# Two feed-forwards of a macaron block: packed expert rows instead of dense passes for five of eight experts

## The chip, the cores and the metric

One core of a Trainium2 chip. The metric is the device time of one execution of the whole program in microseconds (us), median of three runs.

## What is computed

The input x has 8 batches of 512 tokens of 128 numbers, all fp32. Three residual steps follow each other:

```python
x = x + 0.5 * ffn(layernorm(x))
x = x + attention(layernorm(x))        # 16 heads of 64
x = x + 0.5 * ffn(layernorm(x))        # the same weights again
```

The feed-forward has two shared experts, which every token passes, and eight routed ones, of which each token uses two. An expert keeps at most 1280 (token, choice) pairs, counted in token order; what comes later is dropped:

```python
scores = softmax(x @ gate_w.T); topk_w, topk_idx = top_k(scores, 2)
topk_w = topk_w / (topk_w.sum(-1) + 1e-20)
keep = pos_tok < capacity                       # capacity = 1280 of 8192 pairs
comb = zeros(N, 8).at[arange(N), topk_idx].add(topk_w * keep)
eo_e = (silu(x @ we_gate_e.T) * (x @ we_up_e.T)) @ we_down_e.T      # for each expert e
y = sum over e of eo_e * comb[:, e]
sh = silu(x @ ws_gate.T) * (x @ ws_up.T) @ ws_down.T
return y + sh
```

## The kernel before

Tokens live in SBUF as `x_tok` (128 partitions are 128 tokens; 8 batches of 4 tiles of 128). Each engine has its own instruction list and runs it in order; semaphores tie them together. `setup_sync` (line 161 on) queues all loads on SP. Then come `ffn("f1")`, `attention()` and `ffn("f2")`, one behind the other on every engine.

The feed-forward (`ffn`, lines 277 to 751) goes batch by batch, and in a batch through ten groups k: the two shared experts and all eight routed ones, each on all 512 tokens, whichever expert a token has chosen. Tokens are transposed once a batch (`front`, L347), so columns are tokens. A group on PE is `gate_up` (L375): six fp32r matmuls of 512 columns. Each fp32 factor is split into a high and a low fp32r part, and three products make one. The gate result goes through silu on ACT (L496), the product with the up result is taken on DVE (`gated`, L635). For a routed expert PE spreads the combine weight of each token over the partitions by one bf16 matmul (`weights`, L410), and DVE multiplies by it (`weighted`, L643). ACT makes the high part of the hidden values (L505), POOL the low part (`hidden_low`, L728), and PE adds three down matmuls (`project`, L418) into one PSUM bank Y that collects all ten groups. At the end of a batch ACT copies Y with the factor 0.5, PE transposes it back (L427) and DVE adds it to `x_tok` (`residual`, L650). `groups` (L307) is the loop over b with k written out; `project` runs four groups late (LAG_Y), so that the other engines keep up.

Layer norm (`norm_stage`, 16 stages, L259 to L265) and routing (`route_stage`, 20 stages, L555 to L616) are chains of small DVE instructions. Tables written by hand (`NORM_AT`, `ROUTE_AT`) lay some stages in each group. Routing of batch b needs logits in token rows: PE multiplies (L355), ACT copies, PE transposes (L362). The top two are found by comparing all pairs of experts (L576 to L586, 256 columns), positions in an expert's queue by matmuls with a triangular matrix (`positions`, L382 to L387). The combine weights are split in three bf16 parts, transposed and kept as `comb_t`.

In the last batch of feed-forward 1, `follow` calls lay the first steps of attention between the groups (`early_pe`, `early_act`, `early_dve`). Attention itself (L851 on) runs in periods of one pair of heads, 64 of them and three before and after. It starts once all eight residuals are done (`ffn1["x_done"]`).

## Time and profile before

| | us |
|---|---|
| median of three runs | 1410.64 (1409.23 to 1411.74) |
| the profiled execution | 1412.86, of which the span from first to last instruction is 1410.8 |
| PE busy, share of the span | 1297.9, 92% |
| DVE | 1000.4, 71% |
| POOL | 926.1, 66% |
| ACT | 703.9, 50% |
| mean granted clock of TensorE | 0.978 of full |

Busy times are those of instructions that compute. Matmuls are pipelined and their ends are modelled: what a matmul costs is better read from the distance of two starts. A name such as `work` or `turn` can stand for several things in turn, since buffers are shared: in the feed-forward `work` holds the hidden values and `qk_h`, `qk_l` their parts.

### The profile page before, as it was taken

To read this page: it belongs to the slowest core of one execution; us is meant where nothing else is said; L and a number is where in the kernel's file an instruction comes from. 1 tells how busy PE (TensorE), PEld (TensorE's weight loads), DVE (VectorE), ACT (ScalarE), POOL (GpSimd) and SP (SyncE) were. 2 spreads that over 40 slices of the span, in tenths; PEclk is the share of its full clock that TensorE was granted. 3 is DMA by queue.
4 is the path that set the end of the run, shared out by engine and by line. 5 is a ranking of instruction groups with operands and counts; after the bars stand their busy time and mean duration, and the time that the engine had idled before them with its cause. 6 is when DMAs were issued, how large, how long until landed. Compare 5 with 4: busy or idle time off the path is not lost.

```text
span 1410.8 us, 25300 instructions
## 1 busy us (share of the span) xinstructions
PE 1297.9 (92%) x8258; PEld 828.9 (59%) x8258; DVE 1000.4 (71%) x1900; ACT 703.9 (50%) x1042; POOL 926.1 (66%) x684
## 2 busy tenths in 40 slices
PE   4999889689999999999999999999999937988997
PEld 2666666346656656666566566566566525666665
DVE  7889988687666666666666666666666426998896
ACT  3565555245455555555555545545545404555553
POOL 0444444577888888888888788788888512444444
PEclk9999999899999999999999999999999967999999
DMA  6000000123233232232232332332332210000000
GB/s 206 1 0 0 0 0 0 30 46 69 48 68 68 48 69 65 51 69 61 55 69 57 59 69 51 65 69 47 69 69 47 39 24 0 8 7 15 7 7 16
DMA packets 101418, 61.71 MB, mean 44 GB/s; under 512 B 75280, under 2 KB 84016, under 8 KB 101072
## 3 DMA queue, kind: packets, MB, share of 16 engines
q1 hardware_dynamic: 101328, 60.52, 19.8%
q8 instruction: 56, 0.92, 0.3%
q14 instruction: 34, 0.28, 0.1%
HBM read 24.30 MB, written 2.62 MB: 19 GB/s over the span
## 4 chain that ended last, share of the span: by engine, by line
PE 68%; DVE 8%; issue 3%; DMA 1%; DVEq 0%; POOL 0%; ACT 0%; SPq 0%; POOLq 0%; ACTq 0%
PE banks L919 16%; PE banks L902 13%; PE banks L934 6%; PE banks L878 6%; PE banks L843 6%; PE banks L907 4%; PE banks L375 4%; PE banks L943 4%; PE banks L862 3%; PE banks L418 2%; PE banks L885 1%; PE banks L410 1%; DVE xn L265 1%; DVE neg_max L1064 1%; DVE work L643 1%
## 5 line engine op out<-in xcount | busy, mean ns | idle before, releaser
L728 POOL TENSOR_TENSOR qk_l<-work,qk_h 128x512 fp32r<-128x512 f32 x160 | 206.3, 1293 | 301.2 <-ACT qk_h L505 299.8
L1064 DVE TENSOR_REDUCE neg_max<-banks 128x2 f32<-128x1024 f32 x256 | 313.4, 1224 | 102.5 <-PE banks L878 96.3
L1000 ACT ACTIVATE work<-banks 128x1024 f32<-128x1024 f32 x256 | 250.1, 1025 | 168.3 <-PE banks L907 168.3
L1148 POOL TENSOR_TENSOR turn<-turn,side_turned 128x512 f32<-128x512 f32 x128 | 160.7, 1276 | 129.1 <-DMA side_turned<-side 129.1
L919 PE MATMUL banks<-work 128*64 128x512 f32 x1024 | 233.8, 598 | 0.0
L1142 POOL TENSOR_TENSOR turn<-turn,fenc 128x512 f32<-128x512 f32 x128 | 162.4, 1291 | 12.6 <-DVE side L1057 8.9
L1153 POOL TENSOR_TENSOR qk_l<-turn,qk_h 128x512 fp32r<-128x512 f32 x128 | 162.1, 1289 | 0.9 <-ACT qk_h L1005 0.9
L1158 POOL TENSOR_TENSOR work<-work 128x1024 f32<-128x1024 f32 x64 | 153.1, 2392 | 6.2 <-PE banks L919 6.2
L919 PEld LDWEIGHTS banks<-work 128*64 128x64 f32 x1024 | 67.8, 136 | 132.8 <-issue 110.0
L505 ACT ACTIVATE qk_h<-work 128x512 fp32r<-128x512 f32 x160 | 100.6, 629 | 71.5 <-DVE work L643 62.1
L375 PE MATMUL banks<-x_hi,gu_hi 128*128 (+1 forms) x320 | 133.5, 417 | 2.6 <-DVE work L635 2.2
L375 PE MATMUL banks<-x_hi,gu_lo 128*128 (+1 forms) x320 | 128.9, 403 | 0.0
L375 PE MATMUL banks<-x_lo,gu_hi 128*128 (+1 forms) x320 | 127.6, 399 | 0.0
L878 PE MATMUL banks<-qk_h 64*128 64x512 f32 x512 | 116.7, 452 | 11.3 <-DVE neg_max L1064 8.3
L496 ACT ACTIVATE o_t<-banks 128x512 f32<-128x512 f32 x160 | 94.7, 592 | 63.8 <-PE banks L375 54.0
L1070 DVE TENSOR_TENSOR shift<-banks,own_rows 128x512 fp32r<-128x512 f32 x64 | 44.2, 691 | 111.0 <-PE banks L885 111.0
L643 DVE TENSOR_TENSOR work<-turn,banks 128x512 f32<-128x512 f32 x128 | 87.4, 684 | 35.2 <-PE banks L410 29.1
L1005 ACT ACTIVATE qk_h<-turn 128x512 fp32r<-128x512 f32 x128 | 80.5, 629 | 53.6 <-POOL turn L1148 53.5
L902 PE MATMUL banks<-qk_h 64*128 64x512 f32 x512 | 101.9, 395 | 1.4 <-DVE side L1057 1.4
L1057 DVE TENSOR_TENSOR turn<-banks,rope_t 128x1024 f32<-128x1024 f32 x63 | 77.1, 1224 | 36.6 <-PE banks L843 35.5
L902 PE MATMUL banks<-qk_h,qk_l 64*128 64x512 f32 x512 | 101.3, 392 | 0.0
L902 PE MATMUL banks<-qk_l,qk_h 64*128 64x512 f32 x512 | 101.3, 392 | 0.0
(149 smaller groups left out, 2517.6 us busy)
## 6 DMA issues: line engine op xcount, KB each, us to landing
side_turned<-side SPq DMA_DIRECT2D x256, 128.0 KB, 3.1
rec_all<-rec_d SPq DMA_DIRECT2D x128, 128.0 KB, 3.0
x_tok<-in_x SPq DMA_DIRECT2D x8, 256.0 KB, 5.8
out<-x_tok SPq DMA_DIRECT2D x8, 256.0 KB, 2.3
work<-in_w_gate_up SPq DMA_DIRECT2D x1, 1280.0 KB, 6.6
work<-in_w_qk SPq DMA_DIRECT2D x1, 1024.0 KB, 7.1
den_d<-den_rows SPq DMA_DIRECT2D x64, 4.0 KB
den_c<-den_d SPq DMA_DIRECT2D x64, 4.0 KB, 1.9
```

Of the source, the lines that this page charges most:

```text
L375: ins = nc.tensor.matmul(dst[:], w[:, j + k, :], of_batch(a, b), start=(n == 0), stop=(n == 2))
L643: nc.vector.tensor_tensor(hid[:, k % NH, :], prod[:, k % 2, :], C[k % 2][:], ALU.mult).then_inc(s["hidden"], 1)
L728: nc.gpsimd.tensor_tensor(hid_lo[:, k % 2, :], hid[:, k % NH, :], hid_hi[:, k % 2, :], ALU.subtract).then_inc(s["hid_lo_ready"], 1)
L878: ins = nc.tensor.matmul(M2[:, h, :], qk_h[OWN[h], g % SETS, Q, qt * P:(qt + 1) * P], qk_h[OWN[h], g % SETS, K, :], start=True, stop=True)
L902: nc.tensor.matmul(S[kt][:, h, :], k[OWN[h], g % SETS, K, keys], q[OWN[h], g % SETS, Q, :], start=(i == 0), stop=False)
L919: ins = nc.tensor.matmul(O[OWN[h], :], v_all[:, kt, n * DH:(n + 1) * DH], pt[:, g % 2, kt, h * T:(h + 1) * T], start=(kt == 0), stop=(kt = ...
L1000: nc.scalar.activation(pt[:, g % 2, kt, :], S[kt].rearrange("p h q -> p (h q)"), ACT.Exp, scale=QSCALE).then_inc(s["probs"], 1)
L1064: nc.vector.tensor_reduce(neg_max[:, g % 2, qt::DH], M2, AX.X, ALU.max, negate=True).then_inc(s["maxes"], 1)
L1142: nc.gpsimd.tensor_tensor(turn[:, g % 2, part], turn[:, g % 2, part], fenc[:], ALU.add).then_inc(s["with_fourier"], 1)
L1148: nc.gpsimd.tensor_tensor(turn[:, g % 2, part], turn[:, g % 2, part], side_turned[:, part], ALU.add).then_inc(done, 1)
L1153: return nc.gpsimd.tensor_tensor(qk_l[:, g % SETS, part], turn[:, g % 2, part], qk_h[:, g % SETS, part], ALU.subtract)
L1158: nc.gpsimd.tensor_tensor(pt[:, g % 2, 0, :], pt[:, g % 2, 0, :], pt[:, g % 2, 1, :], ALU.add).then_inc(s["first_sum"], 1)
```

## The change

Shared experts and the routed experts 0 to 2 stay dense, on all tokens. Experts 3 to 7 run on packed rows: the normalised row of each token is written for each of its two choices to a list in HBM (`xs_d`) by an indirect DMA of GpSimd, 128 rows a time, at the place `slot_id` that routing works out; rows that belong to a dense expert or are over capacity get a place beyond the list's end and are not written. Each row carries two more numbers, the row where its result goes and its weight (ROW = 130). SP reads the list of an expert (1280 rows) into `xe`, PE transposes it, and the expert runs in three parts of 512, 512 and 256 columns (`PART_TILES`). ACT scales the result rows by their weights (`move`), GpSimd writes them to `ys_d` by their row numbers (`give_back`), and at the end SP reads `ys_d` back in token order for both choices, and DVE adds both (`combine`). The lists are filled first by SP (`fill`): `xs_d` with rows whose destination is out of bounds, `ys_d` with zeros.

The order of work is a list of 55 units. The first 30 are dense; the last ten dense ones lie two by two ahead of the three parts of each packed expert:

```python
+def ffn_units():
+    dense = [("dense", b, g) for c in range(CHUNKS) for gs in (range(NSH), range(NSH, NSH + DENSE))
+             for b in range(CB * c, CB * (c + 1)) for g in gs]
+    units = dense[:len(dense) - BESIDE]
+    rest = dense[len(dense) - BESIDE:]
+    for k in range(SPARSE):
+        a, b, c = (("sparse", PARTS * k + n, NSH + DENSE + k) for n in range(PARTS))
+        units += [rest[2 * k], rest[2 * k + 1], a, b, c]
+    return units
```

Down products are single fp32 matmuls with the hidden values as weights, so the result stands in token rows; DVE adds it to `x_tok` with 0.5 (shared) or the combine weight (dense experts), and nothing is transposed back. The three-part combine weights, the weight rows and the high and low parts of hidden values and down weights are gone, with POOL's elementwise work. Layer norm and routing take a chunk of two batches at once; the top two are found by two maxima with a tie rule. Logits are taken with the tokens as weights.

```diff
-            def pool(pool):
-                def hidden_low(b, k, before):
...
+                def send(c):
+                    pool.wait_ge(s["xn_twice"], c + 1)
+                    pool.wait_ge(s["routed"], c + 1)
+                    for t in range(CT):
+                        for way in range(TOPK):
+                            nc.gpsimd.indirect_dma_start(
+                                xs, bass.IndirectOffsetOnAxis(slot_id[:, c % 2, way, t:t + 1].bitcast(U32), 0),
+                                rows_out[:, c % 2, way, t, :], None, bounds_check=SPARSE * CAPACITY - 1,
+                                oob_is_err=False).then_inc(sent[c % 2], 16)
+                def give_back(n):
+                    pool.wait_ge(s["y_moved"], n + 1)
+                    for j, t in enumerate(part_tiles(n)):
+                        nc.gpsimd.indirect_dma_start(
+                            ys_d, bass.IndirectOffsetOnAxis(xe[:, n // PARTS % 2, t, D:D + 1].bitcast(U32), 0),
+                            ys[:, n % YS, j * P:(j + 1) * P], None, bounds_check=TOPK * B * T - 1,
+                            oob_is_err=False).then_inc(returned[n % YS], 16)
...
+                def fetch(k):
+                    if k >= 2:
+                        for n in range(PARTS * (k - 1) - YS, PARTS * (k - 1)):
+                            at_least(sp, returned[n % YS], 16 * slot_rows(n))
+                    sp.dma_start(xe[:, k % 2], xs[k * CAPACITY:(k + 1) * CAPACITY]...).then_inc(in_xe[k % 2], 16)
+                def fetch_back(b):
+                    if b >= YIN:
+                        sp.wait_ge(s["x_done"], b - YIN + 1)
+                    for way in range(TOPK): ...   # 256 KB each into y_in
+                for n in range(2):
+                    sp.wait_ge(sent[n], 16 * 2 * CT * (CHUNKS // 2))
+                for k in range(SPARSE):
+                    fetch(k)
+                for n in range(S - YS, S):
+                    sp.wait_ge(returned[n % YS], 16 * slot_rows(n))
+                for b in range(B):
+                    fetch_back(b)
...
-                    for n, (w, a) in enumerate(((down_hi, hid_hi), (down_lo, hid_hi), (down_hi, hid_lo))):
-                        ins = nc.tensor.matmul(Y[:], w[:, k, :], a[:, k % 2, :], ...)
+                    for t in range(width(i) // P):
+                        tok = slice(t * P, (t + 1) * P)
+                        for m in range(summed):
+                            j = summed - 1 - m
+                            ins = nc.tensor.matmul(y_bank(i)[:, tok], hid[:, (i - j) % NH, tok], down_w[:, g - j, :],
+                                                   start=(m == 0), stop=(m == summed - 1))
...
+                def period(i):                     # PE
+                    if i < N:
+                        gate_up(i)
+                    c, q = chunk(i)                # six periods a chunk
+                    if 0 < c < CHUNKS and q == 0:
+                        logits(c)
+                    if c < CHUNKS and q == 4:
+                        positions(c)
+                    if front_at(i) is not None:
+                        front(front_at(i))
+                    if gathered_at(i) is not None: # two units ahead of a packed part
+                        gathered(gathered_at(i))
+                    if 0 <= i - LAG < N:
+                        down(i - LAG)
...
+                def combine(b):                    # DVE
+                    dve.wait_ge(in_y[b % YIN], 32 * (b // YIN + 1))
+                    if b == 0:
+                        dve.wait_ge(s["y_added"], results(N, "dense"))
+                    xb = x_tok[:, b].rearrange("p t d -> p (t d)")
+                    steps.link(tt(xb, xb, y_in[:, b % YIN, 0].rearrange("p t d -> p (t d)"), ALU.add))
+                    tt(xb, xb, y_in[:, b % YIN, 1].rearrange("p t d -> p (t d)"), ALU.add).then_inc(s["x_done"], 1)
```

Comments in this fence mark what the shortened lines are. `setup_sync` queues `fill(sp, 0)` behind the loads of x and `fill(sp, 1)` behind attention's weights, 7.5 MB each, both ahead of feed-forward 1's `fetch`. The weight splits of gate and up are in two halves, the second at unit 4; attention's are in the last units (`early_act`, `early_dve`). Attention's first norm, projection and rotation are laid between the combines of feed-forward 1 (`joined`).

## Rows read from the trace of the kernel before

**Rows 1.** Stretches: us, busy of PE, PEld, DVE, ACT, POOL; clock, DMA share, GB/s.

```profile
0.00:20.00 20.00, 6.93 (x16) 3.29 (x17) 10.23 (x44) 7.58 (x9) 0.20 (x4) 1.00 0.90 279
60.00:260.00 200.00, 178.70 (x829) 127.20 (x828) 174.42 (x490) 108.30 (x184) 89.46 (x70) 1.00 0.01 3
180.16:208.85 28.69, 26.06 (x124) 18.71 (x123) 25.86 (x76) 15.94 (x27) 12.89 (x10) 1.00 0.00 0
600.00:1000.00 400.00, 400.00 (x2959) 243.41 (x2957) 262.64 (x275) 209.37 (x290) 337.03 (x245) 1.00 0.30 61
```

**Rows 2.** Timeline: where the feed-forwards start and end, PE and DVE.

```profile
18.74 0.77 PE L375 MATMUL banks<-x_hi,gu_hi 128*128 128x512 f32 x1 [0.25 <-issue]
...
260.82 0.69 DVE L650 TENSOR_TENSOR x_tok<-banks,x_tok 128x512 f32<-128x512 f32 x1 [5.04 <-PE banks L427]
...
1157.60 0.69 DVE L1084 TENSOR_TENSOR x_tok<-banks,x_tok 128x512 f32<-128x512 f32 x1 [9.27 <-PE banks L943]
...
1170.12 0.63 PE L375 MATMUL banks<-x_hi,gu_lo 128*128 128x512 f32 x1
1170.55 0.63 PE L375 MATMUL banks<-x_lo,gu_hi 128*128 128x512 f32 x1
```

**Rows 3.** DVE timeline, one batch apart: start us, us, engine, line, operation.

```profile
183.32 0.68 DVE L552 TENSOR_TENSOR x_lo<-banks,x_hi 128x512 f32 x1
...
212.01 0.68 DVE L552 TENSOR_TENSOR x_lo<-banks,x_hi 128x512 f32 x1
```

**Rows 4.** PE timeline in feed-forward 1 and in attention.

```profile
180.36 0.40 PE L375 MATMUL banks<-x_hi,gu_hi 128*128 x1
180.60 0.40 PE L375 MATMUL banks<-x_hi,gu_lo 128*128 x1
...
181.06 0.60 PE L347 MATMUL banks<-ident,xn 128*128 128x128 f32 x4
181.42 0.48 PE L375 MATMUL banks<-x_hi,gu_hi 128*128 x1
...
705.78 1.05 PE L943 MATMUL banks<-wo,o_t 128*128 128x128 f32 x8
706.76 0.50 PE L878 MATMUL banks<-qk_h 64*128 64x512 f32 x2
```

**Rows 5.** DVE timeline: small steps and two products of 512 columns.

```profile
204.00 0.19 DVE L604 SCALAR_TENSOR_TENSOR route<-banks,route 128x32 f32<-128x32 f32 x1
204.11 0.16 DVE L606 TENSOR_TENSOR count<-count,tile_n 128x8 f32<-128x8 f32 x1
...
254.51 1.28 DVE L643 TENSOR_TENSOR work<-turn,banks 128x512 f32<-128x512 f32 x2
```

**Rows 6.** Waits, 60 to 260 us: total, times, longest.

```profile
DVE work L643 <- PE banks L410: 14.2, 21, 1.4
```

**Rows 7.** Timeline of DVE in the batch, and POOL beside L577.

```profile
191.53 0.71 DVE L241 TENSOR_SCALAR rsi<-ve 128x4 int32<-128x4 int32 x1
...
194.86 1.53 DVE L577 TENSOR_TENSOR rec_all<-route 128x256 f32<-128x256 f32 x1
...
198.37 0.42 DVE L582 TENSOR_TENSOR rec_all<-rec_all 128x256 f32<-128x256 f32 x1
...
205.90 1.80 DVE L265 TENSOR_SCALAR xn<-x_tok,mean,rs 128x128 f32 x4
...
194.82 1.28 POOL L728 TENSOR_TENSOR qk_l<-work,qk_h 128x512 fp32r<-128x512 f32 x1 [0.17 <-ACT qk_h L505]
```

**Rows 8.** DMAs: count, KB each, median us to landing; one issue on SP.

```profile
side_turned<-side SPq DMA_DIRECT2D x256, 128.0 KB, 3.1
...
x_tok<-in_x SPq DMA_DIRECT2D x8, 256.0 KB, 5.8
out<-x_tok SPq DMA_DIRECT2D x8, 256.0 KB, 2.3
...
2.26 0.43 SPq L166 DMA_DIRECT2D work<-in_w_gate_up  x1
```

More of the change, by code:

```diff
@@ L466, in pe @@
                 after_attention(pe)
                 pe.wait_ge(in_first, 32)
[L468 removed]
+                for b in range(CB):
+                    front(b)
                 pe.wait_ge(w_lo_ready, 1)
[L470 to L478 removed]
+                logits(0)
@@ L687, in end, with period @@
-                def end(b):
-                    weighted(b - 1, GROUPS - 1)
-                    residual(b)
+                            norm_stage(steps, norms[n], c_norm)
+                def period(i):
+                    if i < N:
+                        gated(i)
+                    if not last and i == REST_AT:
+                        gate_up_low(dve, 1)
+                    c, q = chunk(i)
+                    if c < CHUNKS:
+                        norm_and_route(NORM_AT[q] if c < CHUNKS - 1 else (), c + 1, ROUTE_AT[q], c)
+                    j = i - LAG - 1
+                    if 0 <= j < N and UNITS[j][0] == "dense" and result(j):
+                        if UNITS[j][2] == NSH:
+                            routed.wait()
+                        add(j)
+                    if front_at(i) is not None:
+                        x_low(front_at(i))
+                    if gathered_at(i) is not None:
+                        gathered_low(gathered_at(i))
+                    if follow:
+                        follow["vector"](dve, i - (N - 1 - PAIRS - 2))
```

927 lines of the change are left out of this document (463 added, 464 removed).

## Prediction, made before the change was run

> **What bounds the kernel now.** I read the table by stretches first [rows 1]. The program has three stages: feed-forward 1 up to the last residual at 260.8 us, attention up to the residual at 1157.6, feed-forward 2 from there to the end at 1410.8 us [rows 2]. In attention PE is busy for all of the 400 us shown, and the change leaves those loops alone. In the feed-forwards nobody is at 100%: PE 89% and DVE 87% of 60 to 260 us. So I took one batch out by the distance of two equal instructions, 183.32 to 212.01 us: 28.7 us for ten experts [rows 3]. Its PE busy time of 26.1 us overstates PE, since matmul ends overlap. By starts, an fp32r matmul of 512 columns takes 0.24 us (180.36 to 180.60) [rows 4]; one expert is six of them for gate and up, three for down, and for eight of ten experts one more for the weight row: ten experts are 98 x 0.235 = 23 us, with front, logits and transposes some 25 us. DVE is busy 25.9 of 28.7 us, and its busy time is nearly true: two 128x512 products in 1.28 us [rows 5]. DVE and PE alternate: the longest wait of DVE on PE comes to 14.2 us of 200, for the weight rows [rows 6], which themselves wait for DVE's combine weights once a batch. Hence removing work from PE alone would give little; the change has to shorten both, and it does.
>
> A part of DVE's time is no work. L577 took 1.53 us where L582, the same shape with both operands in SBUF too, took 0.42, and POOL's L728 runs from 194.82 to 196.10 beside it [rows 7]. Six groups are so hit in the batch, L241 first and the four L265 last: 0.5, 0.5 (L576), 1.1, 0.7, 0.8 and 0.7 us over their like, 4.3 in all.
>
> **PE after the change, per feed-forward.** 80 expert passes of 512 columns become 40 dense and 15 packed ones (ten of 512, five of 256). Gate and up: 50 x 6 x 0.235 = 70.5 us, and 30 half-width ones at half of that, 3.5. Down is one fp32 product per 128 rows, 160 + 50 = 210 of them; the form is L943's, whose four products (x8 in the trace) take 0.98 us from 705.78 to the next line's start [rows 4]: 210 x 0.245 = 51.5. Transposes: 24 + 50 at 0.09 (four in 0.36 us) [rows 4] = 6.7. Logits with the tokens as weights: 72 in the loop, 24 ahead; no row has this form, so between 0.06 (half an L943 product's pass) and 0.245; I take 0.12, one of L943's two passes: 9. Changes between fp32r and fp32 cost 0.09 each time, 5. Sum 146 us against some 200 before.
>
> **DVE after, per feed-forward.** A 512-column product costs 0.60 us by starts (1.28 for two, the last of them 0.68) [rows 5], one of 256 columns 0.34 (L582's 0.42 less the same overlap). Gated 50 x 0.60 + 5 x 0.34 = 31.7; the 64 weighted products go. Added: 96 scaled adds of 128x128 at 0.21 (between 0.11 for 32 columns and 0.60 for 512) = 20, eight shared adds 4.8, fifteen low parts 7.7, x_low 4.8. Norm and routing run once per two batches: 28 steps with 8 statistics, and 35 steps of up to 128 columns; a step of 32 columns is 0.19 us busy and 0.11 from start to start where something else fills the gap [rows 5], so 3.8 and 6 us a chunk, 39 for four. Sum 109 us. Since POOL's elementwise work is gone, so is the 4.3 us a batch. Both remain below PE, but in the first 24 periods, which hold all routing, PE has 2.46 a unit (six times 0.235, four times 0.245 and one change) plus (9 + 2) / 24 for logits and fronts, 2.9, and DVE 2.7, one behind the other at times: I take 3.1 us a period, 75 us, then six dense periods at 2.46: sparse work is wanted 91 us after the first matmul.
>
> **POOL and the lists, the unknown.** POOL sends 64 lists of 128 rows and returns 50. No row of before has such a DMA. Nearest from below: SP's issue of a plain DMA, 0.43 us; from above, issue to landing, 2.3 us for a 256 KB store and 3.1 for side_turned, if POOL didn't run ahead of its own transfers [rows 8]. Between lies 1.29 us, what POOL takes to go once through a 128x512 tile [rows 7]. I take 1.2, near POOL's own row, as it is a POOL program that handles 128 rows.
> Beside it, the Trainium skill (DMA: Bandwidth & Descriptors, Anatomy of one DMA) gives about 2.0 us plus bytes/436e3 for a DMA of the gpsimd path, mostly waiting for the receipt; if that held POOL for each list, 2.15 us, an estimate by that page, the sum below would end at 1535 us. No run here shows it yet.
>
> Sends start when chunk 0 is routed, 18 us in: 64 x 1.2 ends at 95 us; the last lists land 2.3 us later, SP fetches 665 KB, 6 us by the 5.8 us landings of x_tok [rows 8]: 103.5. PE wanted it at 91: 12.5 us idle. Then 25 units: 10 dense at 2.46, 10 packed at 2.82, 5 half ones at 1.5, 60 us. fetch(k) waits for the returns of expert k-2 before it reuses its half of xe: two lists, landing and fetch are 10 to 11 us against some three periods of cover, so 3 to 4 us late for three experts, 10. POOL's 50 x 1.2 = 60 us is hidden in these 70. Loop: 91 + 12.5 + 70 = 173.5.
>
> **Both ends.** Start: before, the first gate matmul came 18.7 us into the program, and in feed-forward 2 gate matmuls run 12.5 us after attention's last residual (1170.12), at the lower of the clock's two levels, 0.43 us a matmul from start to start [rows 2]. Now two batches are normalised (0.9 us of statistics more), both fronts share one bank (2.5), and 24 logits products run at the lower level, where copy and turn of the logits fall away (1.5 more): some 2 us more in feed-forward 1, where loads cover part of it, and 5 in feed-forward 2: 20.5 and 16.5. Tail, new: after the last unit, two lists and their landing, 5 us; then 4 MB read back in 16 DMAs at the 279 GB/s of the first 20 us [rows 1], 15 us, landing and last combine 3: 18. In feed-forward 2 the stores share the queue: 6.3 MB, 22.5, landing, combine and the last store 5.5: 28. Feed-forward 1: 20.5 + 173.5 + 5 + 18 = 217 against 261.5. Feed-forward 2: 16.5 + 173.5 + 5 + 28 = 223 against 253.2. Attention's start gains nothing: its first projection moved, but its loop still waits for all residuals. The weight halves, the down low part and the 15 MB of fills lie beside other work; without that cover the fills cost what the rival below says.
> Sum: 44.5 + 30 = 74.5 off the profiled execution's 1412.9 us, which is 2.2 above the median of 1410.6: 1338 us.
>
> **Rivals.** (a) Lists are cheap, 0.43 us: no wait for the sends (12.5 twice), no late fetches (10 twice): 1293 us. For it: SP's price for one issue. Against: POOL's 1.29. Chance 0.10.
> (b) DVE is held by POOL. [rows 7] show that an instruction of DVE with two SBUF operands waits for POOL's to end. If a list holds DVE likewise, POOL now is busy nearly all of the routing phase instead of 45% (12.9 of 28.7 us): 4.3 / 0.45 = 10 us per chain of routing and norm, 40 a feed-forward, of which 10 hide under PE: 30 x 2, 1398 us. For: the same operands. Against: a list reads 128 indices, no tile. The Trainium skill (SBUF — State Buffer, on the shared port pair) agrees with those rows, and adds that DVE's 2-port modes keep GpSimd from writing descriptors, so the hold could go the other way too. The same time comes about if the fills back up: 15 MB with the loads is 22 MB ahead of fetch(0) in SP's queue, 80 us at 279 GB/s, hidden; at half that rate 160 us, 50 us late in feed-forward 1 alone, 1388. Chance of the two 0.25.
> (c) Slower: a list costs over 1.6 us on POOL. Then POOL is the only engine that counts, 114 lists in a row: each 0.1 us adds 6.4 us to the sends and, from 1.4 on, 5 to the returns, twice. 2 x (64 x (c - 1.2) + 50 c - 70) = 75 at c = 1.62; at the 2.3 us of issue to landing it gives 1568 us. Chance 0.17.
> (d) The change does not do what it says: packed passes save nothing because every expert is run at full capacity anyway. But 1280 rows are 2.5 passes of 512 instead of 8, by construction; only stalls could eat it all. Chance 0.03, 1413 us.
>
> **How the numbers follow.** The forecast, a list at 0.9 to 1.35 us, 1315 to 1360 us, has 0.45; so faster by over 0.2% is 0.45 + 0.10 + 0.25 = 0.80, within 0.2% (about what can be told from no change here) 0.03, slower 0.17. The range goes down to rival (a), 1295, and up past (b) to a list at 1.7 us, 1430, which leaves out most of (c) and part of (a), 0.2.
>
> **What would show it.** Right: a POOL queue with 64 lists ending some 95 us after the first matmul, PE idle once for 10 to 15 us before the first packed unit, PE idle 20 to 30 us at the end of each feed-forward with SP's queue busy, down products at 0.245 us, dense periods of 2.5 us once routing is over. Wrong: lists of over 1.6 us; PE waiting in each packed unit for returns; routing steps of DVE at over 0.5 us during sends; dense periods over 3.5 us; fetch(0) landing long after its issue in feed-forward 1 only.

## The result: 1477 us, slower where faster was forecast

The changed kernel took 1476.8 us (median of 4 runs, 1475.1 to 1478.3) against 1411.2 for the kernel before in the same measurement: 1.046 times as long, 95% interval 1.044 to 1.049. The forecast was 1338 us with a range up to 1430, so it missed by 139 us, sign and range both. (The forecast's sum, 1412.9 - 74.5, is at the level of the profiled execution; taken down by the 2.2 us that it names, the median's forecast would be 1336.)

The page's first parts, as the profile of the changed kernel has them (span; busy time by engine; PE, DVE and granted clock in 40 slices), and its two groups of lists (line, operation, count, busy us, mean ns, idle before):

```profile
span 1475.8 us, 22971 instructions
PE 1212.4 (82%) x8234; PEld 819.3 (56%) x8234; DVE 840.6 (57%) x1602; ACT 623.0 (42%) x982; POOL 941.9 (64%) x752
...
PE   5669657169999999999999999999999747696570
...
DVE  4647324487666666666766666666666226573233
...
PEclk9879878569999999999999999999999958897785
...
L767 POOL DMA_INDIRECT xs<-work,slot_id x128 | 124.7, 974 | 180.0 <-DVE slot_id L670 143.4 <-issue 36.5
L775 POOL DMA_INDIRECT ys<-work x100 | 97.9, 979 | 129.0 <-ACT work L548 101.6 <-issue 27.4
```

PE's work fell (1297.9 to 1212.4 us), DVE's too (1000.4 to 840.6). Attention takes 896.8 us from residual to residual, as before. Both feed-forwards now are stretches in which no engine is busy throughout: PE mostly at 50 to 70% in the slices at both ends, at 10% in one, and the clock is down in the same slices.

The timeline of GpSimd in feed-forward 1 shows the skeleton (start us, us, operation, idle before it and who ended it). Each row is the first list of a group, but for the three after the first and the last:

```profile
47.98 1.10 POOL L767 DMA_INDIRECT xs<-work,slot_id  x1 [47.53 <-DVE slot_id L670]
49.38 0.97 POOL L767 DMA_INDIRECT xs<-work,slot_id  x1 [0.30 <-issue]
50.66 0.97 POOL L767 DMA_INDIRECT xs<-work,slot_id  x1 [0.30 <-issue]
...
85.66 0.97 POOL L767 DMA_INDIRECT xs<-work,slot_id  x1 [17.44 <-DVE slot_id L670]
...
117.04 0.97 POOL L767 DMA_INDIRECT xs<-work,slot_id  x1 [11.20 <-DVE slot_id L670]
...
138.22 0.97 POOL L767 DMA_INDIRECT xs<-work,slot_id  x1 [1.02 <-DVE slot_id L670]
...
180.73 0.97 POOL L775 DMA_INDIRECT ys<-work  x1 [22.40 <-ACT work L548]
...
202.49 0.97 POOL L775 DMA_INDIRECT ys<-work  x1 [9.29 <-ACT work L548]
...
224.34 0.97 POOL L775 DMA_INDIRECT ys<-work  x1 [9.21 <-ACT work L548]
...
245.83 0.97 POOL L775 DMA_INDIRECT ys<-work  x1 [9.03 <-ACT work L548]
...
270.62 0.98 POOL L775 DMA_INDIRECT ys<-work  x1 [0.30 <-issue]
```

A list holds GpSimd for 0.97 us and the next starts 1.28 us after it (49.38 to 50.66). The four groups of 16 sends do not follow one another: GpSimd waits 17, 11 and 1 us for the slots of the next chunk. And returns come in groups of ten, 21.6 us apart, with 9 us of idle GpSimd between groups; only the last twenty follow each other.

Where the rest of the feed-forward begins and ends, on PE and DVE: the first gate matmul, the first transposes of packed rows, the last down products, the first and the last combine.

```profile
25.20 0.77 PE L454 MATMUL banks<-qk_h,gu_hi 128*128 128x512 f32 x1 [1.04 <-ACT fenc L238]
...
164.19 1.08 PE L439 MATMUL banks<-ident,work 128*128 128x128 f32 x4 [13.18 <-issue]
...
255.66 1.58 PE L468 MATMUL banks<-down_w,turn 128*128 128x128 f32 x12 [0.84 <-DVE x_tok L698]
...
276.59 0.69 DVE L707 TENSOR_TENSOR x_tok<-x_tok,work 128x512 f32<-128x512 f32 x1 [21.07 <-DMA work<-ys]
...
295.29 0.69 DVE L708 TENSOR_TENSOR x_tok<-x_tok,work 128x512 f32<-128x512 f32 x1
```

With the same marks in feed-forward 2 (from attention's last residual at 1192.1: first packed transposes at 1342.6, last down products until 1436.9, last list until 1450.4, end 1475.8) the miss can be laid out against the forecast's own sum, in us:

| part | forecast | FF1 | FF2 forecast | FF2 |
|---|---|---|---|---|
| up to the first packed transposes | 20.5 + 103.5 = 124 | 164.2 | 120 | 150.5 |
| packed phase, to PE's last down product | 70 | 93.1 | 70 | 94.3 |
| to the end of the last list | 5 | 14.4 | 5 | 13.5 |
| read back, combine (and store) | 18 | 24.4 | 28 | 25.4 |
| sum | 217 | 296.0 | 223 | 283.7 |

79 and 61 us over, 140 in all: nothing is left to explain outside these rows. The waits of the changed kernel name the two places (engine, line, waited for: us, times, longest):

```profile
ACT shift L532 <- PE banks L439: 94.6, 22, 14.5
...
PE banks L402 <- ACT work L512: 61.7, 14, 11.6
...
PE banks L439 <- DMA work<-xs: 48.5, 6, 9.7
DVE x_tok L707 <- DMA work<-ys: 47.8, 9, 21.1
```

and its DMA issues (KB each, median us to landing) show a fetch of an expert at 4.4 us, a list at 2.2 us and the fills at 13.5 and 22.0:

```profile
ys<-blank SPq DMA_DIRECT2D x2, 4096.0 KB, 22.0
...
xs<-blank SPq DMA_DIRECT2D x10, 650.0 KB, 13.5
work<-xs SPq DMA_DIRECT2D x10, 650.0 KB, 4.4
...
xs<-work,slot_id POOLq DMA_INDIRECT x128, 2.2
...
ys<-work POOLq DMA_INDIRECT x100, 2.2
```

### The profile page after: what moved, and what is told of

It is laid out like the page before. It is cut to its first block, busy times and chain, and to the rows that moved or that the text cites. A ratio compares the mean times of both kernels' runs of the same rounds, so it can differ in the third digit from the quotient of the medians.

```text
span 1475.8 us, 22971 instructions
## 1 busy us (share of the span) xinstructions
PE 1212.4 (82%) x8234; PEld 819.3 (56%) x8234; DVE 840.6 (57%) x1602; ACT 623.0 (42%) x982; POOL 941.9 (64%) x752
## 4 chain that ended last, share of the span: by engine, by line
PE 52%; POOL 17%; issue 15%; DMA 6%; DVE 6%; ACT 3%; SPq 1%; POOLq 0%; DVEq 0%; ACTq 0%
PE banks L987 11%; PE banks L970 9%; PE banks L906 5%; PE banks L1002 4%; PE banks L454 4%; POOL ys L775 4%; PE banks L946 4%; PE banks L975 3%; POOL qk_l L1225 3%; POOL xs L767 3%; PE banks L1011 3%; POOL work L1230 3%; PE banks L468 3%; PE banks L930 2%; DMA work<-xs 2%
## 5 line engine op out<-in xcount | busy, mean ns | idle before, releaser
L767 POOL DMA_INDIRECT xs<-work,slot_id x128 | 124.7, 974 | 180.0 <-DVE slot_id L670 143.4
L775 POOL DMA_INDIRECT ys<-work x100 | 97.9, 979 | 129.0 <-ACT work L548 101.6
L687 DVE TENSOR_TENSOR turn<-o_t,banks 128x512 f32<-128x512 f32 (+1 forms) x110 | 72.6, 660 | 109.2 <-PE banks L454 61.3
L468 PE MATMUL banks<-down_w,turn 128*128 128x128 f32 x840 | 124.3, 299 | 11.6 <-DVE x_tok L698 11.6
L468 PEld LDWEIGHTS banks<-down_w,turn 128*128 128x128 f32 x840 | 117.5, 214 | 19.2 <-issue 16.2
L538 ACT ACTIVATE o_t<-banks 128x512 f32<-128x512 f32 (+1 forms) x110 | 63.5, 580 | 137.6 <-PE banks L454 137.3
L975 PE MATMUL banks<-shift,ones_r 64*128 64x512 f32 x512 | 101.5, 392 | 0.0
## 6 DMA issues: line engine op xcount, KB each, us to landing
xs<-blank SPq DMA_DIRECT2D x10, 650.0 KB, 13.5
```

The lines of the kernel that those rows point to most:

```text
L468: ins = nc.tensor.matmul(y_bank(i)[:, tok], hid[:, (i - j) % NH, tok], down_w[:, g - j, :], start=(m == 0), stop=(m == summed - 1))
L767: nc.gpsimd.indirect_dma_start(xs, bass.IndirectOffsetOnAxis(slot_id[:, c % 2, way, t:t + 1].bitcast(U32), 0), rows_out[:, c % 2, way, t, ...
L775: nc.gpsimd.indirect_dma_start(ys_d, bass.IndirectOffsetOnAxis(xe[:, n // PARTS % 2, t, D:D + 1].bitcast(U32), 0), ys[:, n % YS, j * P:(j ...
```

## What the runs gave, in one table

Measurements of kernels with indirect lists fell into two kinds, and no number below can be read without knowing which. In one kind, A, the trace has a landing time for each list, as above. In the other, B, the issue rows of the lists have none, and in all of them but t2 PE, ACT and DVE stand for 5 to 14 us at a time while lists run ("standing" below). A chip always gave one kind, but each chip was used in one session only, so chip and session are not told apart. n1, n2, s1, s2, t1 and t3 bring no token row to its place and back: their times say what waits and work cost, their results are not the program's.

| kernel | median us | ratio to before | kind |
|---|---|---|---|
| changed kernel, first measurement | 1476.8 | 1.046 | A |
| c3_after: the same | 1474.9 | 1.045 | A |
| c1_after, c2_after: the same | 1540.6, 1537.9 | 1.092, 1.087 | B |
| e1_xe3, e2_order, e3_rows3, e4_latefill | 1513.7, 1508.2, 1533.9, 1543.8 | 1.073, 1.069, 1.089, 1.093 | B |
| e5_all / e7_all: the four edits together | 1518.1 / 1384.0 | 1.077 / 0.981 | B / A |
| e6_ring: e1 and e2 together | 1413.2 | 1.002 | A |
| n1_nolists | 1329.2 | 0.941 | no list |
| n2_xe3_plain | 1341.5 | 0.951 | no list |
| s1_standin, s2_standin_all | 1473.5, 1419.2 | 1.044, 1.005 | no list |
| t1_beside | 1503.7 | 1.064 | B |
| t2_loops | 1431.7 | 1.013 | B |
| t3_dose | 1360.6 | 0.963 | A |
| d1_dense | 1424.5 | 1.009 | no list |

## Four edits, each aimed at one wait

My reading of the trace (theory A of these runs) was that the miss consists of separate waits, each of which an edit can take away. e1 gives the fetched rows a third buffer:

> Three buffers for the fetched expert rows instead of two, so that a fetch waits for the returns of the expert three back and not two back; nothing else. Theory A (a ring of waits): in the changed kernel the packed experts follow each other every 21.6 us because ten lists (10 x 1.28 us), their landing (2.2), the fetch (4.4) and the transposes lie in series. With a third buffer the ring is open, experts should follow each other at POOL's ten lists, about 13 us, and the last expert's lists should end some 5 us after PE instead of 11: 4 x 8.6 + 5 us for each feed-forward, so about 1400 us. Rival B (the lists' price itself holds the stage): POOL already is the bound and the spacing stays at 20 us or more, about 1470 us. Rival C (the three result buffers bind next): spacing of 16 to 18 us, about 1435 us.

```diff
-        xe = work[:, 3072:3072 + 2 * 10 * ROW]...
+        xe = work[:, 3072:3072 + 3 * 10 * ROW]...      # and k % 2 -> k % 3, fetch(k) waits for k - 3
```

e2 changes the order of work on PE and ACT in a period:

> Same buffers, another order within a period: PE issues the down products before the front transposes and before the transposes of fetched rows, ACT moves a finished part before it copies the fetched rows. Theory A (head of line): the first part of an expert, four of ten lists, can be returned while the next fetch is awaited, so the spacing of experts falls from 21.6 by 5 us to 16.5, and down products cover part of PE's waits for normalised rows: some 25 us a feed-forward, about 1425 us. Rival B (what stands behind the waiting instruction does not matter): within 5 us of the changed kernel, 1472 us or more.

```diff
+                    if 0 <= i - LAG < N:
+                        down(i - LAG)
                     if front_at(i) is not None:
                         front(front_at(i))
                     if gathered_at(i) is not None:
                         gathered(gathered_at(i))
-                    if 0 <= i - LAG < N:
-                        down(i - LAG)
```

(and `move` ahead of `gathered_high` on ACT). e3 gives the rows to be sent a third buffer, e4 moves the second fill behind attention's transfers:

> A third buffer for outgoing rows, so that chunks 2 and 3 are normalised without a wait for the lists of the chunk two before. Theory A: the waits of ACT on these lists (10.0 and 7.1 us in feed-forward 1, 1.7 and 8.5 in feed-forward 2) go, with a little for the clock that falls behind them: 30 to 35 us, about 1443 us. Rival B: the lists of the last chunk now queue behind those of the chunk before on POOL and the gain is lost there: 10 us or less, 1467 us or more.

```diff
-                    if b % CB == 0 and c >= 2:
-                        act.wait_ge(sent[c % 2], 16 * 2 * CT * (c // 2))
+                    if b % CB == 0 and c >= 3:
+                        act.wait_ge(sent[c - 3], 16 * 2 * CT)
```

(and DVE's wait for the buffer likewise)

> The second feed-forward's lists are filled after attention instead of ahead of feed-forward 1. Theory A (fills hold up the lists): in feed-forward 1 the lists of chunk 0 land after 8.5 us, against 2.2 later, since 7.5 MB of fills are under way; without the second fill ACT's first wait falls from 10 to about 4 us: 6 to 10 us, about 1468 us. Rival B: the first fill is what holds them, or the wait is hidden elsewhere: 1475 us or more. Should the fill now collide with feed-forward 2's own start, its first lists would be late, and the time would not fall either.

```diff
-            fill(sp, 1)
...
             att["sync"](sp)
+            fill(sp, 1)
             ffn2["sync"](sp)
```

All four came out far above what was expected, at 1508 to 1544 us. The ring's period did shrink in e1 and e2; ACT's waits for lists, at which e3 and e4 were aimed, do not show in any trace of kind B, the unedited kernel's included, so whether they shrank cannot be read. In e1 the groups of returns are 17.3 us apart, not 21.6:

```profile
204.64 0.97 POOL L775 DMA_INDIRECT ys<-work  x1 [24.57 <-ACT work L548]
...
221.94 0.97 POOL L775 DMA_INDIRECT ys<-work  x1 [4.85 <-ACT work L548]
```

but they start 24 us later, since all groups of sends were 37 to 38 us apart (in the first measurement 38, 31 and 21). There was no control on that chip, and I had compared with a number from another one. The controls came next.

## The control that moved, and lists taken out

> The changed kernel itself, not edited, beside the next three on their chip. In the four experiments before it PE, ACT and DVE stood for 5 to 14 us at a time with nothing that the trace shows to wait for (rows ending in 'issue' or 'remote') while GpSimd issued its lists; the trace of the changed kernel has next to none of that (PEld L468 behind issue 16 us in total). Theory A (the stalls come from the edits: the code or its timing is shifted, and instructions arrive late): this run gives 1477 us as before and no such stall. Theory B (the stalls belong to the chip or to the day): about 1515 us here too, with ACT o_t behind 'remote' for over 100 us.

The same code took 1540.6 us. Its waits have three groups that the first trace has next to nothing of:

```profile
ACT o_t L538 <- remote: 180.9, 30, 13.5
...
PEld banks L468 <- issue: 128.3, 41, 11.0
...
DVE turn L687 <- issue: 88.4, 16, 11.0
...
xs<-work,slot_id POOLq DMA_INDIRECT x128
```

The last is the issue row of its sends: no landing (that of the returns has none either). How the standing looks, in its timelines of PE and ACT; the second group of sends runs from 86.6 to 107 us. Single records of down products (two records make one product) come 0.7 and 2.1 us apart instead of eight in 0.8 us, with nothing that the trace shows to wait for, and ACT's next copy comes after 13.5 us:

```profile
103.06 0.37 PE L468 MATMUL banks<-down_w,turn 128*128 128x128 f32 x1 [1.75 <-issue]
103.78 0.56 PE L468 MATMUL banks<-down_w,turn 128*128 128x128 f32 x1 [0.35 <-issue]
105.88 0.37 PE L468 MATMUL banks<-down_w,turn 128*128 128x128 f32 x1 [1.54 <-issue]
...
109.52 1.09 ACT L538 ACTIVATE o_t<-banks 128x512 f32<-128x512 f32 x2 [13.53 <-remote]
```

So theory A of that expectation (the edits shift code) fell, and theory B (it belongs to the chip or to the day) stood, though at 1541 and not its 1515 us. Beside 1539 us, the mean of the two controls of kind B, e1 gained 26 us and e2 31, e3 5, and e4 lost 4; those controls ran on other chips than the four, so these differences are rough.

> The changed kernel unedited again, on the chip of the next two runs. It took 1477 us in its own measurement and 1541 us as c1_after, with equal instructions; the second trace has 181 us of ACT o_t behind 'remote' and 128 us of PEld L468 behind 'issue'. Theory A (two levels, which belong to the chip or to how the program was loaded): 1477 or 1541 again, within 5 us of one of the two, and at 1477 no such stalls. Theory B (a drift): something between.

1537.9 us on another chip, again no landings: theory A of that text.

> The four edits of e1 to e4 together: a third buffer for fetched rows, down products ahead of the front and the gathered transposes, a third buffer for sent rows, the second fill moved behind attention. If each takes away its wait and nothing else stood in the way: 1477 - 77 (rings) - 27 (row buffers) - 8 = 1365 us. If the stalls at issue take the place of the waits, as in each of the four alone: 1510 to 1550 us, packed experts spaced 17 us instead of 21.6, and chunk lists 37 us apart.

1518.1 us: in kind B the four edits together give 23 us beside c1_after, on the same chip.

> The changed kernel with every GpSimd list left out (a 1-column memset raises the same semaphore in its place, so no row is sent or returned; the packed experts work on the rows of the fill). Everything else stands: fetches, transposes, moves, fetches back. Theory A (lists and their landing are what the packed ring waits for: 21.6 us an expert, 12.8 of them lists): the ring falls to the PE work of some 14 us an expert, 5 x 7.6 x 2 = 76 us less, the sends' waits (27 us) and the tail of the last lists (8 x 2) go too: 1477 - 76 - 27 - 16 = about 1358 us. Theory B (the rest of the packed phase and the routing on DVE and PE set the pace): over 1430 us.

```diff
-                            nc.gpsimd.indirect_dma_start(xs, ..., rows_out[:, c % 2, way, t, :], ...)
-                                .then_inc(sent[c % 2], 16)
+                            nc.gpsimd.memset(scrap[:, k:k + 1], 0.0).then_inc(sent[c % 2], 16)
```

The same is done to the returns. 1329.2 us: without lists the change is faster, with its fills, fetches, packed passes and the 16 DMAs back all in place. The whole loss hangs on the lists. It is not proof that the rest was well sized, though: the forecast's own figure for lists that hold nobody up, rival (a), is 1293 us, 36 less.

> e1_xe3 with every list replaced by one plain DMA of as many bytes on the same GpSimd queue (100 rows of 520 bytes each way out, 128 rows of 512 bytes back, to fixed places, so the rows are not the experts' own). Theory A (the stalls at issue come from lists, whose descriptors GpSimd makes row by row while it runs): no stalls, and as the list price goes too, about 1370 us. Theory B (the stalls come from shifted code, or from any DMA traffic of GpSimd): ACT o_t stays behind 'remote' for over 100 us and the time stays near 1514.

```diff
-                            nc.gpsimd.indirect_dma_start(xs, ..., rows_out[:, c % 2, way, t, :], ...)
+                            nc.gpsimd.dma_start(xs[row:row + 100], rows_out[0:100, c % 2, way, t, :])
```

1341.5 us on a chip of kind B, without standing. The groups of GpSimd's plain DMAs in it:

```profile
L768 POOL DMA_DIRECT2D xs<-work x128 | 71.0, 563 | 182.7 <-DVE slot_id L670 182.4 <-issue 0.3
...
L774 POOL DMA_DIRECT2D ys<-work x100 | 53.3, 541 | 88.5 <-ACT work L548 87.6 <-issue 0.9
```

0.56 us each and no 0.30 us between them: less than half of a list's 1.28. As many bytes moved by GpSimd cost 12 us more than none (n1, on the same chip) and make nobody stand; it is the indirect form that costs GpSimd double and, in kind B, costs the others.

## Waiting or standing?

A list can cost in two ways: others wait for it, or they stand while it runs. Three runs took these apart. t1 puts lists where nobody waits for them, t2 puts them beside engines whose code is in loops, s1 keeps GpSimd as busy without any list.

> n1_nolists (1329 us) with the 228 lists put back where nobody waits for them: the semaphores are raised by 1-column memsets first, then GpSimd issues as many indirect lists of the same size from a constant tile to DRAM rows that nothing reads. In the first feed-forward back to back as in the changed kernel, in the second with a 768-column memset between two lists. What is left out: as in n1, no token row is sent or returned. Theory A (lists slow the other engines' supply of instructions while they run, whoever waits): stalls at issue on PE, ACT and DVE in the first feed-forward, which is 25 to 60 us longer than in n1, and fewer in the second. Theory B (a list costs only those who wait for it): 1329 to 1335 us and no stall.

```diff
+                    for m in range(2 * CT):                 # after the memsets that raise the semaphores
+                        nc.gpsimd.indirect_dma_start(junk_x, ...row_id[...], blank[:, 0:cols], ...)
```

1503.7 us in kind B, 174 above n1, with ACT behind "remote" for 78.1 us and PEld L474 behind "issue" for 72.1. Feed-forward 1 is 93 us longer than n1's (GpSimd's first attention step at 313.1 against 219.8 us). Theory A as to the sign; the size is beyond it. Part of it is not standing: raising a semaphore still queues behind the lists of the chunk before. In feed-forward 2, where lists have pauses, there is hardly any standing, PE waits 38.0 us for fetched rows (nothing in n1), and still 81 us are lost. The run does not isolate standing as cleanly as it was meant to.

> The kernel before, whose feed-forwards run in hardware loops on PE, ACT and DVE, with one list of 128 rows of 520 bytes (constant tile to DRAM rows that nothing reads) after each of 64 hidden_low steps of GpSimd in the first feed-forward (GpSimd's own code unrolled there and in the second). GpSimd has 1.28 + 1.28 us of work in a group of 3.0 us. Theory A (the stalls are instructions that arrive late, and code in a loop needs none to arrive): 1411 us within 4 us and no stall at issue. Theory B (lists stop the engines by another way, a memory port or the semaphores): PE's rows get holes beside the lists, and the time is 20 us or more over 1411.

```diff
+                    if not last and 2 <= k:
+                        nc.gpsimd.indirect_dma_start(junk_x, ...row_id[:, n:n + 1]..., blank[:], ...)
```

1431.7 us in kind B. No wait of PE, ACT or DVE behind "issue" or "remote" is longer than 1.4 us, yet feed-forward 1 is 20.7 us longer (282.3 against 261.6 at GpSimd's first attention step). So neither theory has it whole: beside looped code there are no stalls of 5 to 14 us, but 64 lists cost 19 us. The lists sit between two steps of GpSimd that PE's down products wait for; that this is the 19 us was not tested, nor what unrolling GpSimd's own code does.

> The changed kernel with each list replaced by two 608-column memsets of GpSimd (about 1.28 us together, as long as a list from start to start), the second of which raises the list's semaphore. What is left out: no token row is sent or returned. Theory A (waiting): GpSimd's time in the chain fetch, PE, ACT, lists, fetch sets 21.6 us an expert less the landing of 2.2, and that and the sends make up most of 76 us a feed-forward: about 1450 us. Theory B (standing at issue makes up most of it): under 1390 us, though GpSimd is as busy as with lists.

```diff
-                            nc.gpsimd.indirect_dma_start(...).then_inc(sent[c % 2], 16)
+                            nc.gpsimd.memset(pad[:], 0.0).then_inc(half_sem, 1)      # 608 columns
+                            pool.wait_ge(half_sem, halves[0])
+                            nc.gpsimd.memset(pad[:], 0.0).then_inc(sent[c % 2], 16)
```

1473.5 us: within 3.3 us of the changed kernel in kind A, without a single list, row or landing. Its groups of returns are 21.4 us apart; the second row begins one stand-in, the third the next:

```profile
173.84 0.60 POOL L769 MEMSET pad<- 128x608 f32 x1 [21.38 <-ACT work L549]
...
195.28 0.60 POOL L769 MEMSET pad<- 128x608 f32 x1 [7.51 <-ACT work L549]
...
196.66 0.60 POOL L769 MEMSET pad<- 128x608 f32 x1
```

This is the run that decides, but not to 3 us. A stand-in came out longer than a list: ten take 13.9 us (195.28 to 209.20), 1.40 each for 1.28, and 1.39 in the sends. Against that it has no landing of 2.2 us. In the ring the two pull against each other, 1.2 us an expert more and 2.2 less, and that the sum comes so close is partly luck. If all 228 stand-ins lay on the path, their extra 0.12 us would be 27 us at most (an estimate). So between 117 and 144 of the 148 us between n1 and the first measurement are GpSimd's time in a chain in which others wait for it; the landings and whatever else a list does are the rest.

> s1_standin with the two edits of the ring (third buffer of fetched rows, down products and moves ahead of the gathered transposes). Theory A: what the ring costs goes, 4 to 5 us an expert: 40 to 50 us under s1_standin. Theory B: within 15 us of s1_standin, as there is little waiting to take away.

1419.2 us, 54 less. Theory A: the ring can be opened.

> n1_nolists (1329 us) with lists that nobody waits for, spread evenly: two lists after each unit's gating in the first feed-forward (110 lists, 2.6 of about 3.3 us), one in the second (55 lists, 1.3 of 3.3 us). What is left out: as in n1. Theory A (standing grows with the share of time in lists, over a reserve of instructions that a pause refills): the first feed-forward 40 to 90 us longer than n1's, the second under 15 us. Theory B (each list costs the engines a fixed piece of time): 0.7 us a list as in t1_beside (81 us for 114 lists), so 75 us and 38 us.

```diff
+                for i in range(N):
+                    pool.wait_ge(s["gated"], i + 1)
+                    for m in range(1 if last else 2):
+                        junk(...)
```

1360.6 us, 31 above n1, in kind A: 23 in feed-forward 1 and 11 in feed-forward 2. Both theories' figures missed, and the 0.2 us a list that comes out is no price of standing: the memsets that raise the semaphores queue behind the lists here too. The last group of sends is raised at 132.8 us instead of 121.0, and PE waits 12.2 us for fetched rows in feed-forward 1 where it waits for none in n1. Its lists of feed-forward 1 had to wait for the fill and then came back to back, and nobody stood. Busy time from 48 to 72 us (us, then PE, PEld, DVE, ACT, GpSimd with counts, clock, DMA share, GB/s), first of t3, then of c1_after:

```profile
48.00:72.00 24.00, 17.44 (x113) 14.84 (x113) 15.27 (x78) 8.89 (x14) 18.43 (x35) 0.93 1.18 225
```

```profile
48.00:72.00 24.00, 12.82 (x73) 10.82 (x71) 6.89 (x32) 6.08 (x8) 15.66 (x16) 0.79 1.18 243
```

19 lists among GpSimd's 35 instructions and 78 instructions of DVE in the one, 16 lists and 32 in the other: a burst of lists alone makes nobody stand. It takes kind B.

## The edits again, beside a control of kind A

> The changed kernel unedited, a third time. Theory A (two kinds of measurement, told apart by whether the trace shows a landing time for lists): with landings, about 1477 us and no standing at issue on PE, ACT and DVE in the feed-forwards; without, about 1540 us with it. Theory B (no such link): landings shown and 1540 us, or none and 1477 us.

1474.9 us with landings of 2.2 us: theory A, and the level of the first measurement, two microseconds off.

> The changed kernel with the two edits of the ring (third buffer of fetched rows; down products and moves ahead of the gathered transposes), with its lists. Beside a control at 1477 us: s2_standin_all's gain of 54 us, so 1420 to 1430 us. Beside a control at 1540 us: about 1500 us, as e1 and e2 alone gave 1514 and 1508 there.

1413.2 us, 61.7 below the control. s2 had said 54.

> The four edits together again. Beside a control at 1477 us: the ring's 54 us, 27 us of waits for row buffers and a few for the late fill, so 1390 to 1410 us, which would be level with or just under the kernel before (1411 us). Beside a control at 1540 us: 1518 us as e5_all.

1384.0 us: 0.981 of the kernel before in the same measurement, 95% interval 0.977 to 0.984. The forecast's sign comes true once the four edits are in. GpSimd in its feed-forward 1:

```profile
47.91 1.10 POOL L770 DMA_INDIRECT xs<-work,slot_id  x1 [47.46 <-DVE slot_id L673]
...
71.20 0.97 POOL L770 DMA_INDIRECT xs<-work,slot_id  x1 [3.08 <-DVE slot_id L673]
...
93.74 0.97 POOL L770 DMA_INDIRECT xs<-work,slot_id  x1 [2.40 <-DVE slot_id L673]
...
158.16 0.97 POOL L778 DMA_INDIRECT ys<-work  x1 [20.34 <-ACT work L549]
...
221.82 0.98 POOL L778 DMA_INDIRECT ys<-work  x1 [0.30 <-issue]
```

Chunks follow at 23 us (the fourth starts at 117.7), and the 50 returns run through from 158.2 to 222.8 us, 1.29 us each: now GpSimd itself sets the packed phase. But on a chip of kind B the same code takes 1518 us.

## The other parts of the change alone

> The two other parts of the change without the first: all eight experts on all tokens, fp32 down products into token rows, routing two batches at once, no row sent, no list, no fill. PE per batch: ten gate and up pairs of 1.4 us, one shared down of 1.62 us and eight expert downs of 0.81 us = 22 us; DVE per batch: ten gatings of 0.69, eight adds of 1.12, and some 5 us of small steps = 21 us. Eight batches, 25 us of start and 15 us of end and routing: some 220 us a feed-forward against 262 and 253 before. Theory A (the lists are what costs, the rest gains): 1310 to 1350 us. Theory B (DVE and PE alternate, as before): 1390 to 1420 us.

```diff
-DENSE = 3
+DENSE = E            # and no fill, send, list, fetch or combine
```

1424.5 us, 12 slower than before; theory B's range was nearly met, but not by its mechanism. The windows (columns as above) show the engines alternating only while routing runs, and PE without a gap afterwards:

```profile
85.00:105.00 20.00, 15.50 (x108) 13.35 (x108) 15.26 (x66) 8.97 (x17) 0.00 (x0) 0.97 0.00 1
...
145.00:165.00 20.00, 20.00 (x125) 17.66 (x124) 14.97 (x44) 5.40 (x9) 0.00 (x0) 1.00 0.00 1
```

Behind routing a dense unit takes 2.29 us, so a batch comes to some 22.7 us where it took 28.7 [rows 3], and that gain is lost again: gate matmuls start at 25 us instead of 18.7 [rows 2], all routing is pressed into 24 units at the front, and attention's first steps on GpSimd wait for the last residual of all batches (266.0 us; 261.6 before). Down products and routing in pairs do not pay by themselves here; what they give beside the packed experts no run separates.

## Why the prediction was wrong, step by step

Three rows of n1 tell what the lists cost and what else was mis-sized: its first and last group of sends and, on PE, its first packed transposes.

```profile
46.84 0.59 POOL L769 MEMSET scrap<- 128x1 f32 x16 [46.41 <-DVE slot_id L671]
...
121.01 0.30 POOL L769 MEMSET scrap<- 128x1 f32 x7 [21.74 <-DVE slot_id L671]
...
134.37 0.60 PE L440 MATMUL banks<-ident,work 128*128 128x128 f32 x4
```

- **Price of a list: right.** I took 1.2 us; it is 1.28 from start to start. By the forecast's own formula that adds 2 x 64 x 0.08 = 10 us and nothing more. Rival (c) asked for over 1.6 us, so its condition was not met, and yet its sign came true. Nor did rival (a) hold (0.43 us), nor (b): DVE's steps of 64 columns take 0.21 to 0.23 us beside lists, no list took over 1.10 us, and the fills, issued by 68 us and landed by about 87, were long through when the first fetch was issued at 159.7. Two of the prediction's signs did show: PE waiting for returns in the packed units, which stood under "wrong", and under "right" one idle time of PE of 10 to 15 us ahead of the first packed unit, 13.2 us, by luck, as both what it waits for and when PE asks for it came about 40 us later than in the sum.
- **"3 to 4 us late for three experts, 10": the step that failed.** I counted the landing and fetch, 10 to 11 us, against three periods of cover. There is no cover. PE runs `gathered(k+2)` ahead of `down(k+1)`, and ACT `gathered_high` ahead of `move`, in program order; so the fetch of expert k+2, which waits for the lists of expert k, holds back the moves of expert k+1, and with them its lists. Ten lists (12.8 us), landing (2.2), fetch (4.4), transposes and a move then form one closed ring of 21.6 us an expert, where PE's work is 12 (n1's returns come every 12.0 us). That is 23 and 24 us in the packed phases and 9 in each tail, as the last expert's ten lists, not two, still stand behind PE: 65 us. s1 reproduces it without a list (21.4 us), and in e6 the 50 returns run through; its 62 us include what the new order gives to the sends.
- **"Sends start when chunk 0 is routed ... 64 x 1.2": failed in the same way, and half of it is the next item.** I laid the 64 sends end to end. Between first and last group lie 90.2 us in the trace, not 57.6: 33 too many in feed-forward 1. n1, in which nobody waits for a list, still has 74.2 between them (46.84 to 121.01). So 17 of the 33 us come from longer periods, the next item, and 16 from lists that are waited for. Up to the first packed transposes the lists cost 29.8 us (164.2 against 134.4) and 24.7 in feed-forward 2 (150.5 against 125.8), where the sum had 12.5: 17 and 12 too few. A chunk's rows need a buffer whose lists must have landed (up to 8.9 us beside the fills), ACT's token rows wait for it, PE's fronts for ACT (61.7 us, against 36.8 in n1), and routing for those. I had named nobody that waits on `sent` in ACT and DVE. With the third buffer, the late fill and the new order the groups are 23 us apart in e7. The first group also came 4.8 us later after the first gate matmul than I took, and that matmul 4.7 us later.
- **"3.1 us a period ... wanted 91 us after the first matmul": mis-sized.** In n1, which waits for no list, the first packed transposes start at 134.4 us, 109 after the first gate matmul, and 107 after it in feed-forward 2 (1136.4 to 1243.7). The fetch is hidden: PE is busy for all of 115 to 134.4 us. That is 18 and 16 us too few for my 91. With the later starts (4.7 and 1.9 us) this makes 41; n1 lies 36 above rival (a), since the end of feed-forward 2 gives 8 back (24.6 us behind PE's last product, for 33).
- **The last list to the end: 24.4 for 18 in feed-forward 1, 25.4 for 28 in the other.** Small, and of both signs. With it the miss is complete: 65 for the ring and its tails, 29 for lists ahead of the packed phase, 34 for the periods, 7 for the starts, 4 here, 139 of 140 us.
- **Down products: right in kind.** The four of a dense unit take 0.81 us from start to the next line's start (55.67 to 56.48 us), 0.20 each, for 0.245.
- **What e7 leaves of the miss.** 1384 - 1338 = 46 us; in feed-forward 1, 30: up to the first packed transposes 20 (of which 9 are the first list's later start, the rest gaps and price), packed phase with its last lists 79.2 for 75, and 6.6 at the end. With the ring open my term of 75 us is right within 5, but then by GpSimd's 50 lists and not by PE's 60 us: partly luck.
- **What I should have asked:** not how long a list is, but what must be finished before its buffer is used again, and what stands behind that wait on each in-order engine. The prediction priced rival (c) as if GpSimd could only hurt by being the busiest engine. It was 64% busy and set the pace by latency. The closed ring was the rival that I lacked. It has 21.6 - 12.8 = 8.8 us outside its ten lists, and I had 14 us for an expert (70 / 5), so it decides from (14 - 8.8) / 10 = 0.5 us a list on (an estimate; with the 12 us of n1, from 0.3), far below the price that I took.

The Trainium skill (DMA: Bandwidth & Descriptors, Anatomy of one DMA) gives 2.0 us plus the bytes for a DMA of GpSimd and says that most of it is the receipt. The landing of 2.2 us agrees with the sum. As to the receipt, GpSimd's own 0.97 us lie within these 2.2 (the last send starts at 157.36 us and the fetch that waits for it is issued at 159.68), so some 1.2 are left for it and the transfer. The reading of it that I had priced at 1535 us, with GpSimd held for all of that, does not: GpSimd is held for 0.97.

## What to carry to other kernels

When a change routes work through an engine that issues transfers, write down the ring (issue, landing, fetch, use, release of the buffer) and walk every in-order queue in it; if one queue serves the next item's arrival ahead of this item's completion, two buffers can give next to no overlap, as here. Replace the suspect by a stand-in of equal length and no effect, and measure the length that it came out with: it told waiting from interference in one run, which four plausible edits had not. And run the unchanged kernel beside every set of edits; against the wrong control the four edits looked like losses, against the right one two of them gained 62 us and all four 91.

## What was not expected of the hardware

- An indirect list of 128 rows costs GpSimd 0.97 us and 1.28 from start to start, a plain DMA of 100 or 128 rows 0.56 and 0.54 us.
- The same program with lists took 1475 and 1477 us in two measurements (chip 4 and one not on record) and 1538 and 1541 in two others (chips 10 and 3); the kernel before (1410.7, 1411.1, 1412.4, 1412.6, 1411.5 us on five chips) did not differ so, and programs without lists were measured on one chip each. In the slower kind PE, ACT and DVE stand during lists, in unrolled code, and the trace lacks the landing of lists. Instructions arriving late would look like this, and the looped kernel did not stand, but nothing here shows the cause. The Trainium skill (Runtime: NRT & Kernel Launch, Instruction fetch mechanics) says that instructions are refilled in blocks of 16 KiB, mostly hidden. The profile's row of that queue agrees on the block (67 packets, 1.10 MB), while single matmul records 0.7 to 2.1 us apart do not look like one late block. What decides the kind is open.
- 110 lists spread over a feed-forward, for whose landing nobody waits, cost 23 us in kind A as well, 55 lists 11 us. The semaphores raised behind them explain part of it (12.2 us of PE behind fetches in the first); whether anything is left for the lists themselves was not tried.
